# Half of the absolute sums of w1 and w2 on VectorE in place of ScalarE, in a two-layer gated cross-attention kernel

## The reference, cut

```
x = x + tanh(g_xattn[0]) * attention(layernorm(x), ctx, Wq, Wkv, Wout)      # 8 heads, rotary, 128 context rows
x = x + tanh(g_ffn[0])   * ternary_ffn(layernorm(x), fast_b, w_fc, w_proj, u, v, gate)   # squared relu
x = x + tanh(g_xattn[1]) * (layernorm(x) @ W[:, :512].T + mean(ctx) @ W[:, 512:].T + b)
x = x + tanh(g_ffn[1])   * quantized_ffn(layernorm(x), w1, b1, w2, b2)      # gelu

def weight_quant(w):                      # for w1 (2048 x 512) and w2 (512 x 2048)
    scale = 1.0 / clip(mean(abs(w)), 1e-05)
    q = clip(round(w * scale), -1.0, 1.0) / scale
```

## Time and profile before

| | us |
|---|---|
| median of 3 runs | 1144.89 |
| lowest, highest | 1142.49, 1146.16 |
| the profiled execution, own time | 1145.46 |
| its span, first to last instruction | 1143.4 |
| TensorE busy | 1086.2 (95%) |
| VectorE busy | 923.9 (81%) |
| ScalarE busy | 798.3 (70%) |
| GpSimd busy | 584.6 (51%) |

### The profile page before, as it was taken

The page is one execution under the profiler, slowest core; times in us unless marked ns, Lnnn a source line. Parts: engine busy times, 40 slices in busy tenths (PEclk is TensorE's granted clock), DMA queues, the critical chain, the costliest instruction groups (busy, mean ns, idle before and its releaser), DMA issues.

```text
span 1143.4 us, 22172 instructions
## 1 busy us (share of the span) xinstructions
PE 1086.2 (95%) x8270; PEld 676.6 (59%) x8558; DVE 923.9 (81%) x1989; ACT 798.3 (70%) x1575; POOL 584.6 (51%) x567
## 2 busy tenths in 40 slices
PE   5776799999999999999999999999999999999997
PEld 5544556475756656474756656565756666564744
DVE  3786788988788797878889888888878777988676
ACT  3988957677685949485876849495775868595634
POOL 1442646564655655556546457463546466564421
PEclk9988799999999999999999999999999999999998
DMA  9779751452534443433335245334343254333110
GB/s 335 239 241 317 232 147 41 95 130 65 120 79 103 98 105 86 100 82 87 93 83 139 61 112 97 86 101 87 89 99 99 54 109 114 75 93 74 38 47 28
DMA packets 273802, 128.11 MB, mean 112 GB/s; under 512 B 247568, under 2 KB 248080, under 8 KB 272016
## 3 DMA queue, kind: packets, MB, share of 16 engines
q1 hardware_dynamic: 273136, 125.73, 43.6%
q10 hardware_dynamic: 560, 0.96, 0.3%
HBM read 57.19 MB, written 8.39 MB: 57 GB/s over the span
## 4 chain that ended last, share of the span: by engine, by line
PE 86%; DMA 4%; ACT 3%; DVE 3%; issue 1%; SPq 1%; POOL 1%; ACTq 0%; DVEq 0%
PE ps L1844 19%; PE ps L1818 18%; PE ps L1887 10%; PE ps L1903 9%; PE ps L1866 7%; PE ps L1771 6%; PE ps L1718 6%; PE ps L1824 2%; PE ps L1758 2%; PE ps L1743 2%; DMA w1T<-in_wcT 1%; PE ps L1611 1%; DMA hT<-q 1%; PE ps L1683 1%; PE ps L1660 1%
## 5 line engine op out<-in xcount | busy, mean ns | idle before, releaser
L1818 PE MATMUL ps<-xT,fcT 128*128 128x256 f16 x2048 | 259.1, 274 | 8.2 <-DMA xT<-x16f 3.9
L732 POOL TENSOR_TENSOR rs<-ve,nhalf 128x1 f32<-128x1 f32 x160 | 102.1, 643 | 283.1 <-DVE ve L1357 207.9
L1844 PE MATMUL ps<-pjT,hid 128*128 128x512 fp8e4 x1024 | 232.1, 379 | 0.0
L1818 PEld LDWEIGHTS ps<-xT,fcT 128*128 128x128 fp8e4 x2048 | 199.1, 98 | 47.1 <-issue 6.5
L759 POOL TENSOR_TENSOR hid<-sq,hid 128x512 f16<-128x512 f32 x128 | 158.6, 1246 | 49.8 <-ACT sq L996 49.3
L1844 PEld LDWEIGHTS ps<-pjT,hid 128*128 128x128 f16 x1024 | 98.3, 98 | 98.9
L949 ACT ACTIVATE e<-ps,nmb,sig 128x128 f32<-128x128 f32 x256 | 113.0, 458 | 7.9 <-DVE nmb L1395 7.8
L985 ACT ACTIVATE rl<-ps,rsf 128x256 f32<-128x256 f32 x256 | 106.5, 469 | 15.6 <-PE ps L1824 14.9
L1887 PE MATMUL ps<-w1T,q4T 128*128 128x512 fp8e4 x480 | 113.4, 379 | 0.0
L764 POOL TENSOR_TENSOR e<-e,einv 128x512 f32<-128x512 f32 x64 | 71.0, 1116 | 74.2 <-DVE einv L1399 73.9
L1903 PE MATMUL ps<-w2T,hT 128*128 128x512 fp8e4 x480 | 108.6, 379 | 0.3 <-DMA hT<-q 0.3
(11 more groups left out here) (243 smaller groups left out, 1987.6 us busy)
## 6 DMA issues: line engine op xcount, KB each, us to landing
xb<-in_x SPq DMA_DIRECT2D x16, 512.0 KB, 4.3
xa<-in_x SPq DMA_DIRECT2D x15, 512.0 KB, 3.9
out<-r SPq DMA_DIRECT2D x30, 256.0 KB, 2.3
rope<-in_rope SPq DMA_DIRECT2D x16, 384.0 KB, 3.5
h<-in_w1T SPq DMA_DIRECT2D x6, 1024.0 KB, 6.4
h<-in_w2T SPq DMA_DIRECT2D x6, 1024.0 KB, 5.9
hid<-in_w_fc SPq DMA_DIRECT2D x2, 1024.0 KB, 8.7
h<-in_wkvT SPq DMA_DIRECT2D x2, 1024.0 KB, 10.3
```

Source lines behind the costliest of these rows:

```text
L732: pool.tensor_tensor(rs[:, n, t:t + 1], ve[:, n, t:t + 1], nhalf[:, :], ALU.pow).then_inc(done, 1)
L1818: pe.matmul(ps[:, FFN0 + m % 2, a * G:(a + 1) * G], fcT[:, k, f * P:(f + 1) * P], xT2[:, xs, k, :], start=(xs == 0 and k == 0), stop=False)
L1844: mm = pe.matmul(ps[:, FFN0 + t, :], hid[:, xs, c, t * P:(t + 1) * P], pjT[:, c, :], start=(c == 0 and xs == 0), stop=(c == FC - 1 and xs ...
```

## The change

The eight sums are shared out. ScalarE keeps the even ones (n = 0, 2, 4, 6), as an activation `Abs` with an accumulated output. VectorE takes the odd ones (n = 1, 3, 5, 7), as one `tensor_reduce` with absolute values each, and counts them on a semaphore of its own, `c_asumd`. TensorE's `mean` waits for four of each, and SP waits for the one that belongs to a piece. To have a semaphore free, `c_rsf` and `c_sc` are merged into `c_bnd` and `c_scd`.

```
-            elif n < W0:
-                eng.wait_ge(c_asum, n - SUM0 + 1)
+            elif n < W0:
+                eng.wait_ge((c_asum, c_asumd)[n % 2], (n - SUM0) // 2 + 1)
...
-                for n in here("ACT", "sums", p):
+                for k in here("ACT", "sums", p):
+                    n = 2 * k
                     arrived(act, SUM0 + n)
                     src = piece[PLACE[SUM0 + n]]
                     act.activation(src, src, ACT.Abs, accum_out=wsum[:, n:n + 1]).then_inc(c_asum, 1)
...
+                for k in here("DVE", "sums", p):
+                    n = 2 * k + 1
+                    arrived(dve, SUM0 + n)
+                    dve.tensor_reduce(wsum[:, n:n + 1], piece[PLACE[SUM0 + n]], axis=AX.X, op=ALU.add,
+                                      apply_absolute_value=True).then_inc(c_asumd, 1)
...
-                    pe.wait_ge(c_asum, 8)
+                    pe.wait_ge(c_asum, 4)
+                    pe.wait_ge(c_asumd, 4)
...
-                     wx=(53,), sums=(39, 40, 41, 44, 45, 46, 47, 49), lift=(55, 56, 64, 67, 74, 79, 81, 83)),
+                     wx=(49,), sums=(39, 41, 43, 44), lift=(51, 52, 60, 63, 70, 75, 77, 79)),
...
+            DVE=dict(sums=(57, 61, 65, 72), x3lo_end=(818, 821), ctx_sum=(14,), rot_k=(8, 9), wq_max=(4,),
```

More of the change, by code:

```diff
@@ L380, in build @@
             DVE=dict(
[L381 to L385, removed]
@@ L400, in build @@
[L400 to L405, removed]
@@ new lines, in build @@
+                rot_lo=((26, 28), (71, 75), (116, 117), (168, 169), (217, 218), (267, 268), (314, 315), (361, 364),
+                        (413, 414), (461, 462), (509, 510), (557, 558), (608, 609), (657, 658), (707, 708),
+                        (755, 756)),
+                rot=((19, 21), (68, 69), (114, 115), (164, 167), (214, 216), (263, 264), (310, 311), (360, 362),
+                     (411, 412), (457, 458), (507, 508), (555, 556), (604, 605), (653, 654), (705, 706), (748, 749)),
+                sum=((35, 38, 42, 43), (81, 88, 89, 97), (122, 124, 134, 139), (172, 176, 183, 185),
[3 rows of a table added]
@@ new lines, in build @@
+                ln2=((59, 67), (112, 113), (156, 157), (201, 202), (254, 255), (301, 302), (350, 351), (396, 397),
+                     (449, 450), (500, 501), (550, 551), (597, 599), (648, 649), (693, 694), (743, 745), (788, 795)),
+                low=((86,), (121,), (163,), (211,), (262,), (312,), (359,), (407,), (459,), (511,), (559,), (607,),
+                     (655,), (701,), (753,), (800,)),
+                q4=((127, 130), (175, 180), (219, 237), (266, 283), (321, 326), (367, 382), (415, 435), (467, 478),
+                    (520, 525), (569, 580), (618, 623), (662, 669), (712, 720), (761, 770), (799, 802), (823, 825)),
@@ new lines, in build @@
+                x2=((104, 107), (150, 161), (198, 204), (241, 259), (297, 306), (345, 357), (389, 401), (440, 453),
+                    (491, 502), (543, 553), (591, 601), (641, 652), (688, 698), (729, 744), (786, 793), (814, 817)),
+                ln1_st=((0, 1), (10, 12), (62, 63), (129, 155), (181, 205), (227, 253), (284, 300), (337, 349),
+                        (380, 400), (430, 445), (473, 497), (531, 546), (571, 596), (627, 645), (689, 699),
+                        (731, 732)),
+                ln1=((2, 3), (11, 15), (66, 73), (132, 159), (186, 209), (231, 256), (292, 304), (339, 352),
+                     (387, 402), (439, 448), (484, 499), (536, 547), (576, 598), (637, 647), (697, 702), (737, 738))),
@@ new lines, in build @@
+            ACT=dict(
+                low_part=((55,), (85,), (113,), (143,), (177,), (209,), (241,), (272,), (305,), (338,), (370,),
+                          (401,), (434,), (464,), (498,), (529,)),
+                up=((61, 62, 64, 65, 67, 68, 69, 73), (89, 90, 91, 92, 93, 94, 96, 97),
[7 rows of a table added]
+                x1_hi=((2, 3), (9, 12), (46, 47), (104, 112), (136, 144), (164, 176), (203, 206), (234, 239),
+                       (270, 271), (300, 301), (327, 333), (360, 365), (388, 398), (427, 430), (463, 467), (491, 492)),
+                rot=((15, 17), (45, 48), (83, 84), (117, 119), (151, 153), (181, 182), (212, 213), (244, 247),
+                     (279, 280), (308, 309), (340, 341), (372, 373), (403, 405), (436, 437), (473, 474), (497, 501)),
+                exp=((23, 24, 26, 27), (53, 54, 56, 59), (87, 88, 98, 99), (122, 123, 130, 131),
[3 rows of a table added]
+                p_hi=((25, 28, 31, 32), (57, 66, 71, 74), (95, 100, 101, 103), (124, 129, 133, 134),
[3 rows of a table added]
+                pv=((33, 38), (72, 76), (105, 106), (137, 138), (169, 170), (200, 201), (232, 233), (264, 265),
+                    (296, 297), (329, 330), (361, 362), (393, 394), (424, 425), (456, 457), (488, 489), (520, 521)),
+                x2_hi=((42, 50), (81, 82), (110, 111), (140, 141), (174, 175), (204, 205), (237, 238), (268, 269),
+                       (302, 303), (334, 335), (366, 367), (399, 400), (431, 432), (461, 462), (494, 495), (525, 527)),
+                low=((58,), (86,), (114,), (145,), (178,), (211,), (242,), (273,), (306,), (339,), (371,), (402,),
+                     (435,), (465,), (499,), (530,)),
+                x3_hi=((78, 80), (108, 120), (142, 147), (172, 183), (208, 214), (236, 243), (266, 275), (299, 310),
+                       (331, 343), (368, 375), (397, 407), (428, 438), (459, 466), (490, 502), (524, 528), (543, 544)),
+                gelu=((102, 109), (135, 146), (168, 173), (199, 207), (231, 240), (263, 274), (295, 304), (328, 336),
+                      (359, 364), (391, 396), (423, 429), (455, 460), (487, 496), (518, 523), (536, 541), (547, 548)),
+                q5=((107, 115), (139, 149), (171, 179), (202, 210), (235, 248), (267, 278), (298, 307), (332, 337),
+                    (363, 369), (395, 404), (426, 433), (458, 470), (493, 500), (522, 526), (539, 542), (549, 550))),
@@ L1228, in hidden_scale @@
                 dve.wait_ge(c_bnd, 6)
-                dve.tensor_scalar(rsf[:, :], scf[:, :], rho[:, :], None, ALU.mult).then_inc(c_rsf, 1)
+                dve.tensor_scalar(rsf[:, :], scf[:, :], rho[:, :], None, ALU.mult).then_inc(c_bnd, 1)
             def mix_row():
@@ L1335, in prepare @@
                     dve.wait_ge(d_rows, 32)
-                    dve.tensor_scalar(scbc[:, :], ps[:, 0, :], c1[:, :], None, ALU.mult).then_inc(c_sc, 1)
+                    dve.tensor_scalar(scbc[:, :], ps[:, 0, :], c1[:, :], None, ALU.mult).then_inc(c_scd, 1)
                     dve.tensor_scalar(b2bc[:, :], b2bc[:, :], tg[:, 3:4], None, ALU.mult).then_inc(c_b2, 1)
```

94 lines of the change are left out of this document (32 added, 62 removed), and 58 rows, old and new, of tables (exp, h, max, p_hi).

## The result

| | before | changed |
|---|---|---|
| median of 14 runs each, us | 1144.32 | 1147.22 |
| lowest, highest | 1142.49, 1147.2 | 1144.43, 1148.3 |
| span of the profiled execution | 1143.4 | 1146.2 |

The ratio is 1.0025, with a 95% interval from 1.0016 to 1.0034: the changed kernel is about 2.9 us slower, just inside the 0.3% that the prediction took as its bound. The forecast was 1.8 us.

The account below looks back on a forecast made before the run. TensorE, 95% of the span, bounds the kernel, so the start's end at about 144 us decides. rot_hi +1.95 us, less some return, taken as +1.8 on the median 1144.89, gives 1146.7 us; range 1144.0 to 1149.8.

Parts of the forecast that it names:

- what replaces sum 7: Group 2's second layer norm, behind sum 7 on VectorE, delays x1_hi, then rot_hi of group 1 to 113.35: +1.95 us.
- VectorE's steps: Four added sums, 8.9 us against 7.9 idle, move VectorE's steps between 90.6 and 112.7 us step by step.
- the price of the first rot_lo: First rot_lo of group 1 on VectorE moves +1.0 us, from 108.51 to 109.5, ahead of sum 7.
- what was to come back: ScalarE's 0.26 us wait at 121.98 vanishes, taking +1.95 to +1.8; GpSimd's shorter subtraction returns up to 1.0 on its leg.
- The slower rival: SP's held load of the last w2 piece lands late, delaying sum 7; 1149.5 us; chance with a later clock 0.17.
- Kept to the end: A delay or gain TensorE has when leaving the start at about 144 us stays to the end.
- a difference behind 200 us: Sign of being wrong: a time difference arising after 200 us, which nothing in the prediction explains.

Follow-up runs that it names:

- sums 1 and 3 alone: Against the kernel before, VectorE takes only sums 1 and 3 and ScalarE keeps 5 and 7; ratio to the kernel before 1.0005.
- sum 7 alone: Against the kernel before, VectorE takes only sum 7 and ScalarE keeps the other sums; ratio to the kernel before 1.0009.
- ScalarE's gaps used: Two versions of the kernel before, sums all on ScalarE, other steps moved into its waits, the second with lift and rounding later; ratios 1.0011 and 1.0000.
- norm first: Changed kernel with VectorE's sum 7 behind the layer norm of group 2's second tile, second rot_lo directly after; ratio to the kernel before 1.0031.
- x2_hi early: Changed kernel with ScalarE's x2_hi of group 0, second tile, moved up into its wait behind sum 6; ratio to the kernel before 1.0039.
- sum 7 first: Changed kernel with sum 7 one place earlier on VectorE, ahead of group 1's first rot_lo; ratio to the kernel before 1.0025, median 1146.74 us.

## Why the prediction was right, and where it was short

**What bounds, and what replaces sum 7: right, and shown.** The wait that the edit aims at grew; x1_hi waited for the layer norm, rot_hi for x1_hi. Doubling sum 1 showed that VectorE's list has no slack, and the splits that sums 1 and 3 alone cost nothing and sum 7 alone 1.1 us.

**VectorE's steps: right up to rot_lo.** x1_out at 92.75, statistics at 99.75, sum 5 at 102.87, rotations at 105.97 and 107.24 against forecast 92.75, 99.8, 102.9, 106.1 and 107.4.

**Failed: the price of the first rot_lo.** The prediction moved it by 1.0 us and left its duration at 0.69. It took 1.10, beside GpSimd's additions, and that carries sum 7, the norm and rot_hi: 1.95 us forecast, 2.36 measured, and 0.41 is the difference. The section of the Trainium skill's "SBUF — State Buffer" that the prediction cited ("Who interferes with whom") also says that a VectorE tensor_tensor with both inputs in SBUF contends with a GpSimd operation that reads SBUF. The prediction used the section for GpSimd's subtraction and didn't ask it of rot_lo, which its own order put beside GpSimd. The trace agrees with it, 1.10 to 1.12 us beside the additions and 0.68 behind them, and with what it says of reductions, 2.27 us in both places.

**Failed: what was to come back.** The sum took 0.15 us off the 1.95, for ScalarE's wait of 0.26 us. That wait did vanish, and GpSimd's subtraction did shorten (2.14 to 1.64 us, first up pass only +1.86). But ScalarE then waited 1.00 us for TensorE ahead of the first relu, 0.61 before, and the relu was 2.4 us later. TensorE's clock was at the lower level longer (windows of 2 us: busy of each engine, granted clock, DMA share, GB/s), against the earlier trace rows:

```profile
128.00:130.00 2.00, 2.00 (x12) 1.42 (x10) 1.96 (x5) 2.00 (x5) 0.68 (x1) 0.50 0.72 295
130.00:132.00 2.00, 2.00 (x12) 1.46 (x11) 1.90 (x2) 1.00 (x3) 2.00 (x2) 0.55 0.13 38
```

Before, 128 to 130 had 0.87: the clock rose about 3 us later for work that came 2 us later. But this isn't the edit alone. In the second profile of the kernel before, whose work stands 1.4 us earlier, the window 128 to 130 had only 0.58, and ScalarE's wait ahead of the first relu was 1.01 us. Against that profile the changed kernel's shift is 1.93 us at the first exponential and 1.92 at the first relu, against the first one 2.37 and 2.38. From the first exponential to the first relu it took 11.07, 11.09, 11.08 and 11.08 us in the four profiles of the two kernels: nothing is given back there.

**The slower rival's mechanism: excluded.** The last piece didn't make sum 7 wait, though its load was issued at 99.86.

**"Kept to the end": right to about a microsecond.** Group 2's q projection is 2.25 us later as a mean of two profiles each, group 15's output projection 3.1 later (951.6 against 948.5), the median time 2.9. Between the first profiles of the two kernels the shift was nearly kept (2.68, then 2.85); between the second ones it grew from 1.83 to 3.37. The prediction named a difference behind 200 us as a sign of being wrong, and this one is not explained. In the experiments, too, such amounts came and went between group 2 and group 15: the kernels with ScalarE's gaps used lost 0.9 and 1.0 us there against the first profile of before. The forecast was 1.8, the measured 2.9; 0.4 of the gap is rot_lo, 0.15 the return that failed to come, and the rest, half a microsecond, is open.

One more thing may be in it, which the data allow and don't show: where SP is done with the transposes early and the pieces land early, as in seven of the experiments (13.9 to 15.5 us), a kernel whose start waits for pieces gains, and the changed kernel, whose start waits for VectorE, doesn't (norm first, x2_hi early and sum 7 first had piece 6 at 15.2 and scores at 25.6 to 27.1 all the same). With the 6.9 us from piece 6 to the scores in the kernel before, an estimate of the shift at the scores is then about 4 us in place of 2.4. Which landings the timed runs had isn't known.

## What to carry to other kernels

Work moved from an engine that waits to one that seems to have room costs what it takes away from the idle time at that very place: count VectorE's idle time between the new step and the next step that someone waits for, not over the span. Before crediting an engine with freed time, look at what ends its waits; ScalarE's ended with a transfer and with VectorE's layer norm, so 8 us taken off it were worth nothing. Before a difference between two profiles is put down to an edit, look whether the transfers that the stretch waits for were issued at the same distance from a fixed step. When a step is slid to another moment, see which GpSimd step it then stands beside.

## What the runs showed of the hardware

A VectorE subtraction of two SBUF tiles, 128x512, took 0.68 us alone and 1.10 to 1.12 when it began inside a GpSimd addition on SBUF, six times out of six. GpSimd's next step, a power on 128x1 that took 0.54 or 0.55 us in the seven other profiles, took 0.99 or 1.00 in the same six profiles. A VectorE reduction of 128x2048 from SBUF took 2.27 us where its first 0.7 us stood beside the same additions, and 2.27 or 2.28 without.

A VectorE rounding (128x2048) and a GpSimd subtraction (128x512) that met each other in the kernel before: with the rounding 0.16 us ahead, 1.29 and 2.14 us; with the subtraction 0.01 us ahead, 2.23 and 1.16. The same unedited kernel did both.

SP's issue of the same two transposes took 6.5 to 9.0 us, and the 1 MB piece whose load stands behind them landed, counted from one fixed step, between 13.9 and 17.1 us. In the kernel before and with sums 1, 3 the scores stand 6.9 us behind that piece (three profiles); those of the changed kernel repeat to 0.01 us.
